# Fused graph attention and two-expert FFN on one core: another prologue, rstd by logarithm and exponential, and transposes and projection moved ahead of attention

## The chip, the core and the metric

The kernel runs on one core of a Trainium2 chip. The core's engines are TensorE (PE in the profile, PEld for its weight loads), VectorE (DVE), ScalarE (ACT), GpSimd (POOL) and SyncE (SP, which here only issues DMAs). Each engine executes its own list of instructions in order, and the lists meet only at semaphores. The metric is the device time of one execution in microseconds; lower is better.

## The reference

64 graphs of 128 nodes with 128 features each. First a graph attention layer, then a feed-forward layer in which each of the 8192 nodes uses its two most likely of 8 experts. Cut to what matters:

```python
h = layernorm(x);  Wh = h @ W                       # W 128 x 128
s1, s2 = Wh @ a1, Wh @ a2
e = leaky_relu(s1[:, :, None] + s2[:, None, :], 0.2)
x = x + softmax(where(adj > 0, e, -9e15), axis=2) @ Wh
h = layernorm(x)
probs = softmax(h @ gate_w + gate_b)                # 8 experts
top2_vals, top2_idx = top_k(probs, 2)
for e in range(8):                                  # weight 0 for experts not chosen
    out += cw[:, e] * (gelu(h @ W1[e] + b1[e]) @ W2[e] + b2[e])
x = x + out
```

## The kernel before

All is float32, in two stages. The **graph stage** (`NG` = 8 groups of `GB` = 8 graphs) does attention, the router, and a sort: every node's row is written to a DRAM table `sorted_rows` in a region for its pair of experts. The **expert stage** (`NT` = 91 tiles of 128 rows) reads 128 rows of one pair at a time, normalises, runs both experts and writes the rows back to their places.

Group g in the graph stage goes through these helpers. TensorE: `turn_x(g)` (eight 128x128 transposes of the input into the PSUM tile `q_ps`), `project(g)` (eight products with `w_ext` into `wh_ps`; it also gives the attention scores' two vectors and the gate's part), `score(g)` (a transpose of the two vectors, then masks and sums s1 + s2 into `q_ps`), `attend(g)` (eight transposes of the probabilities into `q_ps`, eight products with `wh` into `at_ps`), `count_ranks(g)` (places of the rows by counting, into `q_ps`). ScalarE copies each of them out of PSUM: `copy_xT`, `copy_wh` (which multiplies by rstd, the reciprocal standard deviation of the layernorm's input), `copy_s`, `copy_scores`, `copy_probsT`, `copy_rank`; it also does `exp`, `make_mask` and `exp_router`. VectorE: `split_s(g)` (the two vectors as high and low parts, which `score(g)` waits for), `softmax_shift(g)` (leaky relu and row maximum, `leaky` and `row_max`), `row_sums`, `x1` and `gates` (out of `at_ps`), the layernorm statistics (`stats_at_start` for groups 0 to 3, `of_x`, `of_x1`, `norms` in the loop), some twenty small router steps, and `slots`, `sum_slots`, `store_slots`, which give the row's place in the table (`pos`, line 755). GpSimd builds constants, computes rstd by a power of -0.5 (`rstd_of_start`, `rstd_of`, lines 276 and 328), and issues one indirect DMA (a scatter) of 128 rows per graph (`sort_rows`, line 319, 64 in all).

All three large users of `q_ps` share its two banks, so the order of the helpers on TensorE, and the same order on ScalarE, is written out by hand. Round i of the loop is on TensorE (lines 1091 to 1103) `score(i+1)`, `attend(i)`, `count_ranks(i-2)`, `turn_x(i+3)`, `project(i+3)`; on ScalarE (451 to 477) `copy_s(i+1)`, `exp(i)`, `copy_scores(i+1)`, `copy_probsT(i)`, `copy_wh(i+2)`, `copy_rank(i-2)`, `exp_router(i-1)`, `copy_xT(i+3)`, `make_mask(i+2)`; on VectorE (`rows_and_first(i)`, then `softmax_shift(i+1)`, `split_s(i+2)`, `norms_and_second(i)`). Round 0 differs: `score(1)`, `turn_x(2)` and `project(2)` come after `attend(0)`. Round i of VectorE begins with `row_sums(i, 0)` (line 579), which waits for the first three products of `attend(i)`.

The expert stage starts when all 64 scatters have landed (SP waits for `rows_sorted`, line 262) and the table of tiles is there.

Of the kernel before, what the change touches and what calls it, by code (L numbers as in the profile page):

```python
# [9 lines left out]
ALU = mybir.AluOpType  # L10
# [3 lines left out]
P = 128  # L14
# [20 lines left out]
WB = 3  # L35
# [4 lines left out]
def build(nc, x, adj, W, a, gate_w, gate_b, W1, b1, W2, b2, out, sorted_rows):  # L40
# [7 lines left out]
    with ExitStack() as ctx:  # L48
# [52 lines left out]
        minus_mean = sb("minus_mean", [P, GB, 2])  # L101
        rstd = sb("rstd", [P, 2, 2 * GB])
# [62 lines left out]
        rstd_ready = sem("rstd_ready")  # L165
# [43 lines left out]
        LN = 4  # L209
        RT = 20  # L210
# [9 lines left out]
        def _(sp):  # L220
# [21 lines left out]
            sp.dma_start(gb_row[:, :], gate_b.rearrange("(o e) -> o e", o=1).broadcast_to([P, E])).then_inc(gb_loaded, 16)  # L242
            sp.dma_start(experts[:, :, 0:B1], W1.rearrange("e d h -> d e h")).then_inc(experts_loaded, 16)
# [3 lines left out]
            b2_v = b2.rearrange("(o e) d -> o e d", o=1)  # L247
            sp.wait_ge(filled, 2)
            for k in range(3):
                sp.dma_start(b2_raw[32 * k:32 * k + 1, :, :], b2_v).then_inc(b2_loaded, 16)  # L250
            load_x(3)
            load_x(4)
# [20 lines left out]
        def _(pool):  # L273
# [22 lines left out]
            nc.gpsimd.memset(wh[:, :, :, WK:WK + 1], 1.0)  # L296
# [26 lines left out]
            def rstd_of(i):  # L323
                w = GB if i + 4 >= NG else 2 * GB
                pool.wait_ge(ln_step, LN * i + LN)
                if i >= 2:
                    pool.wait_ge(wh_ready, min(i + 3, NG))
                nc.gpsimd.tensor_tensor(rstd[:, i % 2, 0:w], stat[:, 5, 0:w], minus_half[:, 0:w], ALU.pow)\  # L328
                    .then_inc(rstd_ready, 1)

            for g in range(1, 4):
                rstd_of_start(g)
            for i in range(NG):
                if i >= 2:
                    pool.wait_ge(place_step, PL * (i - 1))
                    sort_rows((i - 2) * GB, (i - 2) * GB + 4)
                rstd_of(i)
                if i >= 2:
                    sort_rows((i - 2) * GB + 4, (i - 1) * GB)
            for i in range(NG - 2, NG):  # L340
                pool.wait_ge(place_step, PL * (i + 1))
                sort_rows(i * GB, (i + 1) * GB)
# [9 lines left out]
        def _(act):  # L352
# [14 lines left out]
            def copy_wh(g):  # L367
                act.wait_ge(wh_done, g + 1)
                if g < 4:
                    act.wait_ge(rstd_start_ready, g + 1)  # L370
                    by = rstd_start[:, g, :]
                else:
                    act.wait_ge(rstd_ready, g - 3)
# [44 lines left out]

            def exp_router(g):
# [9 lines left out]

            act.wait_ge(setup_pe, 2)  # L430
# [12 lines left out]
            copy_wh(0)  # L443
            copy_s(0)
            copy_scores(0, 0)
            copy_scores(0, 1)
            copy_xT(1, 0)
            copy_xT(1, 1)
            make_mask(1)

            for i in range(NG):
                if 1 <= i and i + 1 < NG:
                    copy_s(i + 1)
                exp(i)
                if 1 <= i and i + 1 < NG:
                    copy_scores(i + 1, 0)
                    copy_scores(i + 1, 1)
                copy_probsT(i, 0)
                copy_probsT(i, 1)
                if i == 0:  # L460
                    copy_wh(1)
                    copy_s(1)
                    copy_scores(1, 0)
                    copy_scores(1, 1)
                    copy_xT(2, 0)
                    copy_xT(2, 1)
                if i + 2 < NG:
                    copy_wh(i + 2)
# [4 lines left out]
                if i + 3 < NG:  # L473
                    copy_xT(i + 3, 0)
                    copy_xT(i + 3, 1)
# [712 lines left out]
```

## Time and profile before

| | us |
|---|---|
| median of 3 runs (409.86 to 411.43) | 411.04 |
| the profiled execution | 405.03 |
| its span in the trace | 403.0 |

| engine | busy us | share of the span | instructions |
|---|---|---|---|
| PE | 317.4 | 79% | 2354 |
| DVE | 242.9 | 60% | 1003 |
| ACT | 244.7 | 61% | 779 |
| POOL | 187.6 | 47% | 204 |

The graph stage takes the first 188 us or so of the span, the expert stage the rest. The time of an execution is 2.0 us more than the span of its trace. All times below are us from the span's start unless they are marked otherwise. The mean granted clock of TensorE over the span is 0.873 of full speed. In the chain of work that ended last, PE has 49% of the span, POOL 18% (the scatters of line 319 alone 12%, the rstd of line 328 4%) and DVE 11%.

### The profile page before, as it was taken

Reading aid. Unit: us, or ns where it says so; the run is one execution under the profiler, and the core shown is the slowest. Engines: PE = TensorE matmul, PEld = TensorE weight load, DVE = VectorE, ACT = ScalarE, POOL = GpSimd, SP = SyncE. Lnnn points to the kernel's source line nnn. Section 1 sums busy time; section 2 is a strip of 40 time slices with the busy share of each in tenths; the row PEclk is TensorE's granted clock in tenths of the full one; section 3 lists DMA queues with packets and bytes.
Section 4 is the critical chain, followed back from the end, with each engine's and each line's share of the span. In section 5 each row is a group of like instructions: output and inputs, shape, how many; then the busy total and the mean of one; then the engine's idle time right before and its main releaser. Section 6 shows DMA issues by size and latency. Waiting matters only on the chain.

```text
span 403.0 us, 9305 instructions
## 1 busy us (share of the span) xinstructions
PE 317.4 (79%) x2354; PEld 284.4 (71%) x2362; DVE 242.9 (60%) x1003; ACT 244.7 (61%) x779; POOL 187.6 (47%) x204
## 2 busy tenths in 40 slices
PE   7496797798775572210999999999999999999990
PEld 4274675675653461100999999899999999999980
DVE  4226879789788687640266565555566565565550
ACT  3354576576574320001888788787787877888850
POOL 5701410276766578772144444444444444444441
PEclk9868789969896865555899999999999999999996
DMA  7943003246921111111112222222222212212100
GB/s 206 306 124 85 21 0 107 66 119 140 164 50 47 34 36 47 54 55 47 38 46 58 53 59 58 65 57 64 54 69 61 61 47 51 57 51 57 47 3 0
DMA packets 42231, 27.85 MB, mean 69 GB/s; under 512 B 5224, under 2 KB 40070, under 8 KB 42182
## 3 DMA queue, kind: packets, MB, share of 16 engines
q1 hardware_dynamic: 37222, 18.69, 19.8%
q0 software_dynamic: 4960, 8.58, 7.2%
q8 instruction: 22, 0.36, 0.4%
q14 instruction: 27, 0.22, 0.2%
HBM read 16.78 MB, written 12.23 MB: 72 GB/s over the span
## 4 chain that ended last, share of the span: by engine, by line
PE 49%; POOL 18%; DVE 11%; issue 9%; DMA 6%; ACT 3%; SPq 1%; POOLq 0%; ACTq 0%; DVEq 0%
PE at_ps L1149 20%; PE wh_ps L1128 17%; POOL sorted_rows L319 12%; POOL rstd L328 4%; PE at_ps L1147 3%; DMA xt<-sorted_rows 3%; PE q_ps L1118 2%; DMA out_x<-o_sb,xt 2%; PE wh_ps L1018 2%; DVE rows L587 2%; DVE bn L607 1%; DVE bn L615 1%; ACT wh L381 1%; DVE lrelu L560 1%; PE q_ps L1042 1%
## 5 line engine op out<-in xcount | busy, mean ns | idle before, releaser
L346 POOL DMA_INDIRECT out_x<-o_sb,xt x91 | 89.0, 978 | 121.1 <-DVE o_sb L951 119.8
L500 ACT ACTIVATE hid<-wh_ps,pair_w 128x128 f32<-128x128 f32 x364 | 103.6, 369 | 16.9 <-PE wh_ps L1128 16.8
L1149 PE MATMUL at_ps<-experts,hid 128*128 x728 | 111.4, 288 | 0.0
L1128 PE MATMUL wh_ps<-xnT,pair_w 128*128 128x128 f32 x728 | 98.8, 279 | 0.0
L1149 PEld LDWEIGHTS at_ps<-experts,hid 128*128 128x128 f32 x728 | 95.9, 192 | 2.6
L1128 PEld LDWEIGHTS wh_ps<-xnT,pair_w 128*128 128x128 f32 x728 | 90.0, 195 | 0.2
L319 POOL DMA_INDIRECT sorted_rows<-rows,pos x64 | 63.3, 989 | 33.6 <-issue 17.3
L961 DVE COPY pair_w<-experts 128x258 f32 x182 | 54.2, 298 | 31.0 <-issue 18.4
L948 DVE SCALAR_TENSOR_TENSOR o_sb<-at_ps,xt 128x128 f32<-128x128 f32 x91 | 31.9, 351 | 67.3 <-PE at_ps L1149 67.1
L509 ACT ACTIVATE xn<-xt 128x128 f32<-128x128 f32 x91 | 44.5, 489 | 29.5 <-DMA xt<-sorted_rows 29.2
L1147 PE MATMUL at_ps<-experts,ones_bf 65*128 x182 | 40.9, 225 | 2.1 <-ACT hid L500 2.0
L1118 PE MATMUL q_ps<-ident,xn 128*128 128x128 f32 x91 | 25.4, 279 | 15.3 <-ACT xn L509 15.3
L951 DVE SCALAR_TENSOR_TENSOR o_sb<-at_ps,xt,o_sb 128x128 f32<-128x128 f32 x91 | 31.9, 351 | 3.2
L328 POOL TENSOR_TENSOR rstd<-stat,minus_half 128x16 f32<-128x16 f32 (+1 forms) x8 | 18.9, 2356 | 25.9 <-DVE stat L634 25.8
L490 ACT ACTIVATE xnT<-q_ps 128x128 f32<-128x128 f32 x91 | 25.3, 278 | 6.4
L1018 PE MATMUL wh_ps<-w_ext,xT 128*128 128x146 f32 x128 | 18.9, 302 | 8.0 <-ACT xT L364 8.0
L1118 PEld LDWEIGHTS q_ps<-ident,xn 128*128 128x128 f32 x91 | 13.1, 144 | 16.1 <-issue 15.3
L1018 PEld LDWEIGHTS wh_ps<-w_ext,xT 128*128 128x128 f32 x128 | 17.3, 200 | 9.8 <-issue 7.4
L1065 PE MATMUL at_ps<-wh,probsT 128*128 128x139 f32 x128 | 23.3, 351 | 0.3 <-ACT probsT L416 0.2
L1065 PEld LDWEIGHTS at_ps<-wh,probsT 128*128 128x128 f32 x128 | 22.0, 253 | 2.0 <-issue 1.4
L1147 PEld LDWEIGHTS at_ps<-experts,ones_bf 65*128 65x128 bf16 x182 | 18.0, 99 | 4.4 <-issue 4.1
L407 ACT ACTIVATE probs<-lrelu,less_max 128x128 f32<-128x128 f32 x64 | 19.5, 386 | 2.3 <-DVE less_max L565 2.3
(170 smaller groups left out, 390.0 us busy)
## 6 DMA issues: line engine op xcount, KB each, us to landing
xt<-sorted_rows SPq DMA_DIRECT2D x91, 66.5 KB
xin<-in_x SPq DMA_DIRECT2D x8, 512.0 KB, 4.6
adj_sb<-in_adj SPq DMA_DIRECT2D x8, 512.0 KB, 5.4
sorted_rows<-no_row SPq DMA_DIRECT2D x1, 1862.0 KB, 19.0
out_x<-o_sb,xt POOLq DMA_INDIRECT x91
experts<-in_L_ffn_W SPq DMA_DIRECT2D x1, 1024.0 KB, 6.8
experts<-in_L_ffn_W SPq DMA_DIRECT2D x2, 512.0 KB, 8.3
sorted_rows<-rows,pos POOLq DMA_INDIRECT x64
```

The source lines that it names most:

```text
L319: nc.gpsimd.indirect_dma_start(out=sorted_rows, out_offset=bass.IndirectOffsetOnAxis(ap=pos[:, t:t + 1], axis=0), in_=rows[:, t, :], in_of ...
L328: nc.gpsimd.tensor_tensor(rstd[:, i % 2, 0:w], stat[:, 5, 0:w], minus_half[:, 0:w], ALU.pow)\
L346: nc.gpsimd.indirect_dma_start(out=out_v, out_offset=bass.IndirectOffsetOnAxis(ap=xt[:, n % XR, TOK:TOK + 1].bitcast(I32), axis=0), in_=o_ ...
L500: last = nc.scalar.activation(hid[:, n % WR, q, :], wh_ps[:, n % WR, q * P:(q + 1) * P], ACT.Gelu, bias=pair_w[:, n % WR, k, B1 + c:B1 + c ...
L509: nc.scalar.activation(xn[:, n % 2, :], t[:, 0:P], ACT.Identity, bias=t[:, SHIFT:SHIFT + 1], scale=t[:, RSTD:RSTD + 1]).then_inc(xn_ready, 1)
L961: last = nc.vector.tensor_copy(pair_w[:, n % WR, k, :], experts[:, bass.ds(e, 1), 0:W2C])
L1018: last = nc.tensor.matmul(dst[:, o * WE:(o + 1) * WE], xT[:, k, :], w_ext[:, :], start=True, stop=True)
L1065: last = nc.tensor.matmul(dst[:, o * (WK + 1):(o + 1) * (WK + 1)], probsT[:, k, :], wh[:, g % WB, k, :], start=True, stop=True)
L1118: nc.tensor.transpose(q_ps[:, (n % 2) * 512:(n % 2) * 512 + P], xn[:, n % 2, :], ident[:, :]).then_inc(xnT_done, 1)
L1128: last = nc.tensor.matmul(wh_ps[:, n % WR, q * P:(q + 1) * P], pair_w[:, n % WR, k, c * P:(c + 1) * P], xnT[:, n % 2, :], start=True, stop ...
L1147: nc.tensor.matmul(at_ps[:, n % 2, cols], ones_bf[0:65, 0:P], b2_rows, start=True, stop=False)
L1149: last = nc.tensor.matmul(at_ps[:, n % 2, cols], hid[:, n % WR, k * HC + c, :], experts[:, bass.ds(e, 1), W2C + c * P:W2C + (c + 1) * P], ...
```

## The change

In the prologue (groups 0 to 2) the constants are no longer waited for before the statistics of group 1 and before `copy_wh(0)`; `turn_x` and `project` of groups 1 and 2, `score(1)` and group 3's transposes and projection all come before `attend(0)`. In the loop `turn_x(i+3)` and `project(i+3)` stand between `score(i+1)` and `attend(i)`, in every round; `wh` has 4 buffers instead of 3, and `copy_wh(i+3)` follows `copy_probsT(i)`. The power on GpSimd in the loop is replaced: ScalarE takes Ln and Exp (`rough_rstd`), VectorE one Newton step in four small operations (`exact_1` to `exact_4`) between the `x1` of the next round. The table set for Ln and Exp is named at the start and the one for Gelu loaded ahead of the expert stage. The splitting of `b2` goes from VectorE to GpSimd, and on SP the experts' weights are loaded after `x` of groups 3 and 4, `b2` and `adj` of group 2.

```diff
-WB = 3
+WB = 4
@@ sync
+            load_x(3)
+            b2_v = b2.rearrange("(o e) d -> o e d", o=1)
+            sp.wait_ge(filled, 2)
+            ... (three loads of b2)
+            load_adj(2)
+            load_x(4)
             (the three loads of experts)
-            (the three loads of b2), load_x(3), load_x(4)
-            for g in range(2, NG):
+            for g in range(3, NG):
                 load_adj(g)
-                if g + 3 < NG:
-                    load_x(g + 3)
+                if g + 2 < NG:
+                    load_x(g + 2)
@@ gpsimd
-            nc.gpsimd.memset(wh[:, :, :, WK:WK + 1], 1.0)
             for g in range(1, 4):
                 rstd_of_start(g)
-            for i in range(NG):
-                if i >= 2:
-                    pool.wait_ge(place_step, PL * (i - 1))
-                    sort_rows((i - 2) * GB, (i - 2) * GB + 4)
-                rstd_of(i)
-                if i >= 2:
-                    sort_rows((i - 2) * GB + 4, (i - 1) * GB)
-            for i in range(NG - 2, NG):
-                pool.wait_ge(place_step, PL * (i + 1))
-                sort_rows(i * GB, (i + 1) * GB)
+            (a memset and seven operations on b2, from the vector engine's list, each waiting for the last)
+            for g in range(NG):
+                pool.wait_ge(place_step, PL * (g + 1))
+                sort_rows(g * GB, (g + 1) * GB)
@@ scalar
-                if g == 0:
-                    act.wait_ge(consts, 14)          # in copy_wh
+            def rough_rstd(i):
+                w = GB if i + 4 >= NG else 2 * GB
+                act.wait_ge(ln_step, LN * i + LN)
+                nc.scalar.activation(log_var[:, 0:w], stat[:, 5, 0:w], ACT.Ln).then_inc(log_ready, 1)
+                act.wait_ge(log_ready, i + 1)
+                nc.scalar.activation(rough[:, 0:w], log_var[:, 0:w], ACT.Exp, scale=-0.5).then_inc(rough_ready, 1)
+            nc.scalar.preload_act_table_set("natural_log_exp_and_others")
             copy_xT(0, 1)
             make_mask(0)
             copy_wh(0)
+            copy_xT(1, 0)
+            copy_xT(1, 1)
             copy_s(0)
+            copy_wh(1)
             copy_scores(0, 0)
             copy_scores(0, 1)
-            copy_xT(1, 0)
-            copy_xT(1, 1)
+            copy_xT(2, 0)
+            copy_xT(2, 1)
             make_mask(1)
             for i in range(NG):
-                if 1 <= i and i + 1 < NG:
+                if i + 1 < NG:
                     copy_s(i + 1)
                 exp(i)
                 ... (copy_scores(i + 1, 0) and (i + 1, 1))
+                if i == 0:
+                    copy_wh(2)
+                if i + 3 < NG:
+                    copy_xT(i + 3, 0)
+                    copy_xT(i + 3, 1)
                 copy_probsT(i, 0)
                 copy_probsT(i, 1)
-                ... (round 0: copy_wh(1), copy_s(1), copy_scores(1), copy_xT(2))
-                if i + 2 < NG:
-                    copy_wh(i + 2)
+                if i >= 1:
+                    rough_rstd(i - 1)
+                if i + 3 < NG:
+                    copy_wh(i + 3)
                 ... (copy_rank(i - 2), exp_router(i - 1))
-                if i + 3 < NG:
-                    copy_xT(i + 3, 0)
-                    copy_xT(i + 3, 1)
                 ... (make_mask(i + 2))
+            nc.scalar.preload_act_table(ACT.Gelu)
             normalise(0)
@@ vector
+            exact_1: newton0 = stat5 * rough        exact_2: newton1 = newton0 * rough
+            exact_3: newton2 = 1.5 - 0.5 * newton1  exact_4: rstd = newton2 * rough
             def rows_and_first(i):
                 row_sums(i, 0)
+                exact_1(h)
                 x1(i, 0)
+                exact_2(h)
                 x1(i, 1)
+                exact_3(h)
                 x1(i, 2)
+                exact_4(h)
                 row_sums(i, 1)
                 gate_sum(h)
             stats_at_start(0)
+            nc.vector.memset(wh[:, :, :, WK:WK + 1], 1.0)
+            stats_at_start(1)
+            split_s(0)
+            stats_at_start(2)
+            split_s(1)
+            (leaky and row_max of group 0)
+            stats_at_start(3)
             dve.wait_ge(consts, 14)
             dve.wait_ge(gb_loaded, 16)
@@ tensor
             turn_x(0)
             project(0)
-            keep_busy(8)
-            score(0)
+            keep_busy(4)
             turn_x(1)
             project(1)
-            keep_busy(8)
+            score(0)
+            turn_x(2)
+            project(2)
             for i in range(NG):
-                if 1 <= i and i + 1 < NG:
+                if i + 1 < NG:
                     score(i + 1)
-                attend(i)
-                if i == 0:
-                    score(1)
-                    turn_x(2)
-                    project(2)
-                if i >= 2:
-                    count_ranks(i - 2)
                 if i + 3 < NG:
                     turn_x(i + 3)
                     project(i + 3)
+                attend(i)
+                if i >= 2:
+                    count_ranks(i - 2)
```

The waits that guard `q_ps` follow the new order (`turn_x(g)` waits for `copy_scores` of group g-2, `attend(g)` for `copy_xT(g+3)`). `preload_act_table_set` and `preload_act_table` load a table set of ScalarE at that place.

## Rows read from the trace of the kernel before

**Rows 1.** Windows view: length, busy PE, PEld, DVE, ACT, POOL, clock, DMA share, GB/s.
```profile
200.00:403.00 203.00, 191.33 (x1677) 186.36 (x1676) 114.52 (x353) 154.02 (x523) 87.98 (x90) 0.98 0.19 51
```
**Rows 2.** GpSimd's timeline: start, length, operation, in brackets idle before and releaser.
```profile
141.73 0.96 POOL L319 DMA_INDIRECT sorted_rows<-rows,pos  x1 [3.86 <-DVE pos L755]
...
158.35 1.68 POOL L328 TENSOR_TENSOR rstd<-stat,minus_half 128x8 f32<-128x8 f32 x1
...
183.04 0.96 POOL L319 DMA_INDIRECT sorted_rows<-rows,pos  x1 [0.30 <-issue]
184.30 0.96 POOL L319 DMA_INDIRECT sorted_rows<-rows,pos  x1 [0.30 <-issue]
```
**Rows 3.** ScalarE's timeline, start of the expert stage.
```profile
189.63 0.49 ACT L509 ACTIVATE xn<-xt 128x128 f32<-128x128 f32 x1 [13.68 <-DMA xt<-sorted_rows]
...
193.43 1.28 ACT L500 ACT_TABLE_LOAD   x1
...
194.73 1.14 ACT L500 ACTIVATE hid<-wh_ps,pair_w 128x128 f32<-128x128 f32 x4
```
**Rows 4.** VectorE's timeline, first instruction of rounds 0, 1, 4, 5, 6, 7.
```profile
33.37 0.18 DVE L579 RECIPROCAL rowinv<-at_ps 128x3 f32<-128x3 f32 x1 [5.88 <-PE at_ps L1065]
...
58.78 0.18 DVE L579 RECIPROCAL rowinv<-at_ps 128x3 f32<-128x3 f32 x1 [2.26 <-PE at_ps L1065]
...
102.62 0.18 DVE L579 RECIPROCAL rowinv<-at_ps 128x3 f32<-128x3 f32 x1
...
117.15 0.18 DVE L579 RECIPROCAL rowinv<-at_ps 128x3 f32<-128x3 f32 x1 [0.61 <-PE at_ps L1065]
...
134.01 0.18 DVE L579 RECIPROCAL rowinv<-at_ps 128x3 f32<-128x3 f32 x1 [3.86 <-PE at_ps L1065]
...
145.44 0.17 DVE L579 RECIPROCAL rowinv<-at_ps 128x3 f32<-128x3 f32 x1
```
**Rows 5.** VectorE's timeline inside rounds 1 and 4.
```profile
65.01 0.18 DVE L552 TENSOR_TENSOR s_cols<-wh,s_cols 128x16 fp32r<-128x16 f32 x1
...
105.60 0.18 DVE L654 TENSOR_TENSOR rows<-minus_mean,rstd 128x16 f32<-128x16 f32 x1 [1.81 <-POOL rstd L328]
```
**Rows 6.** TensorE's timeline: starts of its blocks (L1006 turn_x, L1034 score, L1057 attend, L978 filler).
```profile
8.14 1.07 PE L1006 MATMUL q_ps<-ident,xin 128*128 128x128 f32 x8
...
11.61 1.89 PE L978 MATMUL q_ps<-ones_bf 128*128 128x512 bf16 x7
...
24.87 1.97 PE L1006 MATMUL q_ps<-ident,xin 128*128 128x128 f32 x8
...
29.34 1.89 PE L978 MATMUL q_ps<-ones_bf 128*128 128x512 bf16 x8
31.07 1.04 PE L1057 MATMUL q_ps<-ident,probs 128*128 128x128 f32 x8
...
51.68 0.27 PE L1034 MATMUL q_ps<-ident,s_cols 128*32 128x128 f32 x1
...
55.22 1.94 PE L1057 MATMUL q_ps<-ident,probs 128*128 128x128 f32 x8
...
124.81 0.40 PE L1034 MATMUL q_ps<-ident,s_cols 128*32 128x128 f32 x1 [5.43 <-DVE s_cols L552]
...
130.57 1.97 PE L1057 MATMUL q_ps<-ident,probs 128*128 128x128 f32 x8
```
**Rows 7.** Busy time and granted clock by stretch, around rounds 1 and 5 (columns as Rows 1).
```profile
38.00:41.90 3.90, 3.90 (x13) 2.71 (x13) 3.46 (x21) 0.60 (x1) 1.93 (x2) 0.51 0.87 238
...
45.10:47.40 2.30, 2.30 (x20) 2.08 (x18) 2.30 (x13) 0.82 (x4) 0.00 (x0) 1.00 0.00 0
...
124.80:130.50 5.70, 4.86 (x14) 3.04 (x15) 5.14 (x37) 3.20 (x10) 3.23 (x4) 0.50 0.13 43
```
**Rows 8.** ScalarE's timeline: the copy of the first projection.
```profile
16.23 2.24 ACT L381 ACTIVATE wh<-wh_ps,rstd_start 128x138 f32<-128x138 f32 x8 [5.30 <-POOL part L315]
```

**Rows 9.** The source view of line 755, the rows' places: durations in ns, first and last start.
```profile
L755 DVE CAST pos<-pos_f x8: 151/152/171, 81.3 to 169.0; 128x8 int32<-128x8 f32 x8
```

More of the change, by code:

```diff
@@ L209, in build @@
         LN = 4
+        RS = 4
         RT = 20
@@ L634, in norms, with exact_1, exact_2, exact_3 @@
                 nc.vector.tensor_tensor(stat[:, 5, 0:w], stat[:, 3, 0:w], stat[:, 4, 0:w], ALU.add).then_inc(ln_step, 1)
+            def exact_1(i):
+                w = GB if i + 4 >= NG else 2 * GB
+                dve.wait_ge(rough_ready, i + 1)
+                nc.vector.tensor_tensor(newton[:, 0, 0:w], stat[:, 5, 0:w], rough[:, 0:w], ALU.mult).then_inc(rstd_step, 1)
+            def exact_2(i):
+                w = GB if i + 4 >= NG else 2 * GB
+                dve.wait_ge(rstd_step, RS * i + 1)
+                nc.vector.tensor_tensor(newton[:, 1, 0:w], newton[:, 0, 0:w], rough[:, 0:w], ALU.mult).then_inc(rstd_step, 1)
+            def exact_3(i):
+                w = GB if i + 4 >= NG else 2 * GB
+                dve.wait_ge(rstd_step, RS * i + 2)
+                nc.vector.tensor_scalar(newton[:, 2, 0:w], newton[:, 1, 0:w], -0.5, 1.5, ALU.mult, ALU.add)\
+                    .then_inc(rstd_step, 1)
+            def exact_4(i):
+                w = GB if i + 4 >= NG else 2 * GB
+                dve.wait_ge(rstd_step, RS * i + 3)
+                if i >= 2 and i + 2 < NG:
+                    dve.wait_ge(wh_ready, i + 3)
+                nc.vector.tensor_tensor(rstd[:, i % 2, 0:w], newton[:, 2, 0:w], rough[:, 0:w], ALU.mult).then_inc(rstd_step, 1)
             m1, k1, total, p1, e2, p2, k2, df, qa, qb, hi, lo, tri, cls = (small[:, j, :] for j in range(14))
@@ L827, in _ @@
             stats_at_start(0)
+            nc.vector.memset(wh[:, :, :, WK:WK + 1], 1.0)
[3 more added lines that the diff above has]
+            split_s(1)
+            for h in range(2):
+                leaky(0, h)
+                row_max(0, h)
+            stats_at_start(3)
             dve.wait_ge(consts, 14)
             dve.wait_ge(gb_loaded, 16)
-            stats_at_start(1)
-            split_s(0)
-            softmax_shift(0)
             for i in range(NG):
@@ L840, in _ @@
                     gates(0)
-                    split_s(1)
-                    stats_at_start(2)
-                    stats_at_start(3)
-                    softmax_shift(1)
+                else:
+                    rows_and_first(i)
+                if i + 1 < NG:
+                    softmax_shift(i + 1)
+                if i + 2 < NG:
+                    split_s(i + 2)
+                if i == 0:
                     for k in range(GB):
@@ L878, in _ @@
             store_slots(NG - 2)
+            exact_1(NG - 1)
+            exact_2(NG - 1)
+            exact_3(NG - 1)
+            exact_4(NG - 1)
             gate_sum(NG - 1)
```

103 lines of the change are left out of this document (38 added, 65 removed).

## The prediction, on record before the changed kernel was run

> **What bounds the kernel now.** I read the chain of work that ended last, then the timelines of the engines on it, then the windows. From 200 us on TensorE is busy 191 of 203 us [rows 1]: the expert stage is TensorE's, the change touches only its first instructions, and I carry it over as it is. It begins when the last scatter has landed: the last is issued at 184.30, and ScalarE waits until 189.63, 13.68 us long, for the first tile that is read back [rows 2, 3]. So the graph stage is worth what the last scatter is worth.
>
> GpSimd issues a scatter every 1.26 us [rows 2], 10.1 us for a group of eight, while the rounds of VectorE take longer: between the rounds' first instructions lie 25.4 us (round 0), 14.6 us on average (rounds 1 to 4), 16.9 (round 5) and 11.4 (round 6) [rows 4]. GpSimd therefore waits for each group's places until group 4, whose places come in round 6 and whose first scatter starts at 141.73, 7.7 us after the round's first instruction at 134.01 [rows 2, 4]. From then on it no longer waits: 32 scatters and two powers of 1.68 us and their issue to the end [rows 2]. So the end of the stage is "start of round 6 plus 50.3 us", and what matters before is how fast the rounds go.
>
> A round is a ring. VectorE's first instruction waits for `attend(i)`; 6.4 us later (58.78 to 65.19 [rows 4, 5]) `split_s(i+2)` is done; that releases `score(i+2)` on TensorE, then `attend(i+1)`, which releases the next round. The second half of the ring is 3.54 us of score (51.68 to 55.22) plus 2.30 us of attend (31.07 to 33.37) at the full clock, and 5.76 (124.81 to 130.57) plus 3.44 (130.57 to 134.01) at the half clock [rows 4, 6]. Meanwhile VectorE has about 7 us of statistics and router work of its own, so in rounds 2 to 4 the two sides are nearly level. `turn_x` and `project` run now beside the first half of the ring, while TensorE waits for `split_s`: they cost nothing.
>
> **The change, part by part.**
>
> *Transposes and projection between score and attention.* They leave the free place and enter the ring. The two blocks take 3.47 us at the full clock (8.14 to 11.61) and 4.47 us at the half (24.87 to 29.34), ScalarE's copies between them included [rows 6]. `attend(i)` is queued behind them, VectorE's round waits for `attend(i)`, everything else for that. This falls on the rings that lead to rounds 1 to 4; the later rounds have no group left to turn. What they leave behind is a hole: TensorE ends `attend` and `count_ranks` some 2.7 us into a round and has nothing until `split_s`.
>
> The clock decides how dear it is. At 124.81 TensorE had idled 5.43 us, and score ran at a granted clock of 0.50, that is 1.2 GHz [rows 6, 7]. Score does not bring it back either: at 38.0 to 41.9 TensorE is busy all the time with score and is at 0.51; transposes and projection follow until about 46, and the full 2.4 GHz is back at 45.1 to 47.4 [rows 7]. In the new order every score follows an idle of about 4.5 us. I take 5.3 us for score (bounds 3.54 and 5.76, nearer the half clock), 4.4 for turn and project (3.47 and 4.47), 2.6 for attend (2.30 and 3.44, the clock mostly back): 12.3 us, bounds 9.3 and 13.7.
>
> *rstd by Ln and Exp.* Two powers after 141.73 leave GpSimd's list, and VectorE's wait for them (1.81 us in round 4 [rows 5], between 0 and that in the others) goes. In their place VectorE has four small operations, at about 0.1 us each from start to start in a stream of such, 0.18 at most [rows 5]: 0.4 us per round. `exact_1` waits for ScalarE, where Ln and Exp (at most 0.28 us each, the mean of the eight copies in [rows 8]) stand behind `copy_probsT(i)`; they end about when VectorE starts its round. Bounds 0 and 0.8 us of stall, queued behind it the `x1` of the round; I take 0.3, since the products that release VectorE come after the same copy. `copy_wh(i+3)` waits for `exact_4`, 1.6 us into the round; behind it wait `copy_rank`, `exp_router` and `make_mask`, all needed only after the first half of the ring. So the first half becomes 6.45 + 0.7 = 7.15 us, and the new round 7.15 + 12.3 = 19.45 against 14.6. VectorE's own list (7.15 + 7) is shorter and is now hidden.
>
> *Prologue.* `copy_wh(0)` sat idle for 5.30 us until 16.23 for constants it does not need [rows 8]; now it can run at 11.85, when `project(0)` is done [rows 6]. But more stands ahead of `attend(0)`. Following TensorE and ScalarE: `copy_wh(0)` to 14.3 (2.4 us with its two small copies), the first half of `copy_xT(1)` 0.6, `project(1)` to 17.1, `score(0)` to 20.9, `turn_x(2)` and `project(2)` to 24.9, half of it at the half clock, `score(1)` to 28.6, `turn_x(3)` waits for `copy_scores(1)`, then ScalarE does `copy_wh(2)` (2.4) before `copy_xT(3)` (0.6 for its first half), `project(3)` from 32.2 to 34.9, attend 2.6: round 0 starts at 37.5. With every block at the full clock it is 36.4, at the half 42.5. Before: 33.37 [rows 4]. Round 0's first half is short (no router), rows 3.0, shift 2.45, split 0.4 = 5.85 us, then 12.3: round 1 starts at 55.65, against 58.78. The prologue gains 3.1 us there, because groups 1 and 2 are ready, not more, since `turn_x(4)` and `project(4)` are in the ring.
>
> *Gelu's table ahead of time.* The load of 1.28 us at 193.43 is on the path [rows 3] and moves into the 13.68 us in which ScalarE waits: -1.3 us. The Trainium skill (ScalarE: Activation LUTs, What ACT_TABLE_LOAD costs) counts 2.66 us per switch with a drain. By the page the gain would be 1.4 us larger. In the trace the activation behind the load starts at 194.73, 0.02 us after the load's end [rows 3], so I keep 1.3.
>
> *b2 on GpSimd, loads in another order, memset, filler.* Nothing. GpSimd's first scatter will not come before about 84 us (the first places came at 81.3 [rows 9]), and between the starting rstd and that it has only b2's eight operations; even at three times 1.68 us each they would end by 70 us. VectorE loses them in round 0, where it idled anyway until 58.78 [rows 4]. All loads that move forward are needed later than they land.
>
> **The sum.** Rounds start at 37.5, 55.65, then three times 19.45: round 4 at 114.0 (before 102.62). Round 5: 7.15 + 9.2 (score and attend at the half clock, as 124.81 to 134.01) = 130.4; round 6 likewise, 146.8 (before 134.01). Group 4's first scatter comes 7.7 + 0.7 = 8.4 us later, and 31 more at 1.263 = 39.15 behind it: the last starts at 194.4, against 184.30 [rows 2]. That is +10.1, less 1.3 for Gelu: +8.8 us. Group 7's places came at 169.0 [rows 9], 35 us into round 6; with 8.9 us to their last scatter's start that is 44 against 47.6, so they don't bind. The profiled execution would take 405.03 + 8.8 = 413.8; the runs' median is 6.0 above it, so I add the same to the median: 411.04 + 8.8 = 419.8 us.
>
> **Rivals.**
> 1. *The clock stays at 2.4 GHz, and the kernel is faster.* Transposes and projections beside score could feed TensorE enough. With all blocks at the full clock: round 0 at 36.4, 1 at 51.6, three rounds of 7.15 + 9.3 to 101, two of 13.0 (VectorE's own work then, 12.6, is nearly level) to 127.0; last scatter 174.6, -9.7, with Gelu -11.0: 400. For it: round 5 began after an attend at the full clock (117.15). Against: the idle of 4.5 us in every round, and score at the half clock even when it is busy [rows 7]. The ring's second half decides: it must be under 10.1 us instead of 12.3 for the change to break even. 10%.
> 2. *The clock comes back in mid-ring more often.* Second half about 10.3 us: round 6 at 139, the end within 2 us of before: 412. 9%.
> 3. *Ln and Exp don't stay in one table set with the sign, copy and exp of the loop.* Then 1.28 us [rows 3] per switch, two a round in ScalarE's list, half of it ahead of `exact_1`: 7 x 1.3 to 2.6 us more, 429 to 438. The Trainium skill (ScalarE: Activation LUTs, Table sets: the hidden batching unit) says one set has both Ln and Exp and that cheap functions are in every set; by it this rival is nothing. 5%.
> 4. *The half clock holds through attend too*: second half 13.7 and a prologue with round 0 at 42.5: +19: 430. The Trainium skill (TensorE: Matmul & The Clock Gate, PE-mode transpose) says transposes don't count as activity for the clock, which would speak for it; the trace shows eight transposes of the input in 1.07 us at one place and 1.97 at another [rows 6], so they at least run at the full clock where it is granted. 6%.
>
> **How the numbers follow.** The forecast, a ring of 11 to 13.5 us and a result of 414 to 427, has 70%. About 0.5% (2 us) is what a measurement of this kernel can tell from no change. Faster by more: 10% (rival 1). Within: 8%, most of rival 2. Slower: 82%. The range reaches down into rival 2 and up short of rivals 3 and 4: 409.5 to 427.
>
> **What would show it.** In the trace after: the first instructions of rounds 1 to 5 should lie 18 to 20.5 us apart; before each `score` TensorE should idle 4 to 5 us for `split_s`, and VectorE 4 us or more before each round for `attend`; score at 0.5 to 0.7 of the clock; round 1 at 54 to 57; no wait of VectorE for rstd over 0.8 us; GpSimd without a wait in its last 32 scatters; a single table load before the experts. It is wrong if the rounds come at 16.5 us or less (clock), if round 0 starts before 35, or if ScalarE loads tables in the loop.

## The result, and the profile after

Over four runs the changed kernel takes 421.24 us (419.73 to 422.48), beside 410.45 us for the kernel before on the same chip (four runs, 405.21 to 411.43). The ratio is 1.031, its 95% interval 1.020 to 1.041: slower, by about 3%. The forecast was 419.8 us with a range of 409.5 to 427.

The traces say more than +10.8 us. The profiled execution of after took 420.99 us with a span of 419.0, against 405.03 and 403.0 of before, so trace to trace it is +16.0 us, where +8.8 had been worked out. The last scatter went from 184.30 [rows 2] to 201.09: +16.8, and -0.8 behind it. The median was met partly by luck, because two errors cancel: the graph stage lost 6.7 us more than predicted, and the profiled execution of before lies 5.4 us below the median of its own runs, while that of after lies on its median.

The page of after, granted clock, the chain and one group:

```profile
PEclk9965775768685656555579999999999999999996
...
PE 61%; DVE 11%; POOL 10%; issue 7%; DMA 5%; ACT 3%; SPq 1%; POOLq 0%; ACTq 0%; DVEq 0%
...
L598 DVE RECIPROCAL rowinv<-at_ps 128x3 f32<-128x3 f32 (+1 forms) x24 | 4.1, 172 | 53.8 <-PE at_ps L1092 53.6
```

TensorE's share of the chain rose from 49% to 61%, GpSimd's fell from 18% to 10%. The third to the twentieth digit of the clock's line (a slice is 10.5 us) lie between 5 and 8: TensorE is rarely at its full speed in the graph stage. The last line is the round's first instruction: VectorE waits 53.6 us in all before this line, for `attend`.

VectorE's timeline of after, the first instruction of rounds 0 to 6, answers [rows 4]:

```profile
40.88 0.18 DVE L598 RECIPROCAL rowinv<-at_ps 128x3 f32<-128x3 f32 x1 [15.02 <-PE at_ps L1092]
59.99 0.18 DVE L598 RECIPROCAL rowinv<-at_ps 128x3 f32<-128x3 f32 x1 [9.37 <-PE at_ps L1092]
80.37 0.18 DVE L598 RECIPROCAL rowinv<-at_ps 128x3 f32<-128x3 f32 x1 [7.51 <-PE at_ps L1092]
100.74 0.18 DVE L598 RECIPROCAL rowinv<-at_ps 128x3 f32<-128x3 f32 x1 [6.75 <-PE at_ps L1092]
121.13 0.18 DVE L598 RECIPROCAL rowinv<-at_ps 128x3 f32<-128x3 f32 x1 [6.83 <-PE at_ps L1092]
137.32 0.18 DVE L598 RECIPROCAL rowinv<-at_ps 128x3 f32<-128x3 f32 x1 [4.07 <-PE at_ps L1092]
153.62 0.18 DVE L598 RECIPROCAL rowinv<-at_ps 128x3 f32<-128x3 f32 x1 [4.07 <-PE at_ps L1092]
```

The starts of rounds 1 to 4, with a transposition and a projection between each two, follow each other at 20.4 us instead of 14.6 [rows 4]; once no group is left to turn it is 16.2 and 16.3. VectorE idles 6.8 to 7.5 us at the end of each of the long ones.

TensorE's timeline of after from one round's start to the next (80.37 to 100.74), the first instruction of each block (L1061 score, L1036 turn_x, L1048 project, L1084 attend), answers [rows 6]:

```profile
87.14 0.28 PE L1061 MATMUL q_ps<-ident,s_cols 128*32 128x128 f32 x1 [4.54 <-DVE s_cols L571]
...
92.78 1.97 PE L1036 MATMUL q_ps<-ident,xin 128*128 128x128 f32 x8
94.68 3.85 PE L1048 MATMUL wh_ps<-w_ext,xT 128*128 128x146 f32 x16
98.37 1.04 PE L1084 MATMUL q_ps<-ident,probs 128*128 128x128 f32 x8
```

And the windows of after over the same stretches: the hole before score, score, turn and project, attend (columns as [rows 1]), which answer [rows 7]:

```profile
83.00:87.00 4.00, 0.00 (x0) 0.00 (x0) 3.97 (x16) 2.65 (x9) 0.00 (x0) 1.00 0.43 129
87.10:92.80 5.70, 4.83 (x15) 3.05 (x16) 5.70 (x38) 3.20 (x10) 2.85 (x3) 0.56 0.38 115
92.80:98.40 5.60, 5.60 (x26) 5.26 (x26) 1.08 (x8) 1.79 (x3) 4.14 (x5) 0.54 0.16 52
98.40:100.80 2.40, 2.06 (x19) 1.85 (x17) 0.06 (x1) 1.40 (x4) 0.96 (x1) 1.00 0.19 57
```

So a ring is 6.77 us to the start of score, 5.64 of score, 5.59 of turn and project, 2.37 to the next round's start: 20.37. TensorE is empty for 4.54 us, then busy for 11 us at little over half its clock, and is given the full clock only where `attend` begins. While it turns and projects, VectorE is busy 1.08 us of 5.60: nothing else is left to do then.

GpSimd's timeline of after, group 4's first scatter and the last, answers [rows 2]:

```profile
161.76 0.95 POOL L325 DMA_INDIRECT sorted_rows<-rows,pos  x1 [6.21 <-DVE pos L796]
...
201.09 0.96 POOL L325 DMA_INDIRECT sorted_rows<-rows,pos  x1 [0.30 <-issue]
```

The last 32 scatters still run without a wait, now 39.3 us from first to last instead of 42.6, since the two powers are gone. The end of the stage is still "start of round 6 and a fixed list", which makes the rounds the thing to explain.

### The profile page after: what moved, and what is told of

Same layout as the page of the kernel before. It is cut to its first block, busy times and chain, and to the rows that moved or that the text cites. A ratio compares the mean times of both kernels' runs of the same rounds, so it can differ in the third digit from the quotient of the medians.

```text
span 419.0 us, 9314 instructions
## 1 busy us (share of the span) xinstructions
PE 327.7 (78%) x2343; PEld 295.8 (71%) x2350; DVE 240.2 (57%) x1028; ACT 248.7 (59%) x795; POOL 177.8 (42%) x203
## 4 chain that ended last, share of the span: by engine, by line
PE 61%; DVE 11%; POOL 10%; issue 7%; DMA 5%; ACT 3%; SPq 1%; POOLq 0%; ACTq 0%; DVEq 0%
PE at_ps L1173 19%; PE wh_ps L1152 17%; POOL sorted_rows L325 7%; PE wh_ps L1048 5%; DVE rows L606 3%; PE at_ps L1092 3%; PE at_ps L1171 3%; PE q_ps L1072 2%; PE q_ps L1069 2%; PE q_ps L1036 2%; DVE lrelu L579 2%; DMA xt<-sorted_rows 2%; PE q_ps L1142 2%; PE q_ps L1084 2%; PE q_ps L1067 2%
## 5 line engine op out<-in xcount | busy, mean ns | idle before, releaser
L325 POOL DMA_INDIRECT sorted_rows<-rows,pos x64 | 61.8, 965 | 101.9 <-DVE pos L796 84.2
L598 DVE RECIPROCAL rowinv<-at_ps 128x3 f32<-128x3 f32 (+1 forms) x24 | 4.1, 172 | 53.8 <-PE at_ps L1092 53.6
L1048 PE MATMUL wh_ps<-w_ext,xT 128*128 128x146 f32 x128 | 27.9, 397 | 3.4 <-ACT xT L375 3.4
L1048 PEld LDWEIGHTS wh_ps<-w_ext,xT 128*128 128x128 f32 x128 | 26.2, 286 | 5.6 <-ACT x_gate L393 3.6
L1061 PE MATMUL q_ps<-ident,s_cols 128*32 128x128 f32 x8 | 2.6, 323 | 27.7 <-DVE s_cols L571 27.7
L1092 PE MATMUL at_ps<-wh,probsT 128*128 128x139 f32 x128 | 22.4, 341 | 1.4 <-ACT probsT L425 1.4
L1092 PEld LDWEIGHTS at_ps<-wh,probsT 128*128 128x128 f32 x128 | 21.0, 243 | 3.0 <-issue 2.8
L1142 PEld LDWEIGHTS q_ps<-ident,xn 128*128 128x128 f32 x91 | 13.2, 145 | 13.5 <-issue 12.6
L1061 PEld LDWEIGHTS q_ps<-ident,s_cols 128*32 128x32 f32 x8 | 0.8, 98 | 29.7 <-DVE s_cols L571 29.7
```

What stands on the lines that cost most here:

```text
L325: nc.gpsimd.indirect_dma_start(out=sorted_rows, out_offset=bass.IndirectOffsetOnAxis(ap=pos[:, t:t + 1], axis=0), in_=rows[:, t, :], in_of ...
L1048: last = nc.tensor.matmul(dst[:, o * WE:(o + 1) * WE], xT[:, k, :], w_ext[:, :], start=True, stop=True)
L1092: last = nc.tensor.matmul(dst[:, o * (WK + 1):(o + 1) * (WK + 1)], probsT[:, k, :], wh[:, g % WB, k, :], start=True, stop=True)
L1142: nc.tensor.transpose(q_ps[:, (n % 2) * 512:(n % 2) * 512 + P], xn[:, n % 2, :], ident[:, :]).then_inc(xnT_done, 1)
```

## Experiments

The theories, as the expectations name them: **A**, the place in the ring (turn and project between score and attention cost their length, and make the hole in front of score in which the clock goes); **C**, the clock alone (the blocks would be nearly harmless if TensorE stayed warm). The other parts of the change are tested one by one. "Before" is always the run of the kernel before on the same chip. Differences between two experiments are of medians, and where no ratio stands they are told with their ranges.

### Only the order undone

```diff
@@ tensor (and ScalarE's list in the same order, with the waits that guard q_ps)
                 if i + 1 < NG:
                     score(i + 1)
-                if i + 3 < NG:
-                    turn_x(i + 3)
-                    project(i + 3)
                 attend(i)
                 if i >= 2:
                     count_ranks(i - 2)
+                if i + 3 < NG:
+                    turn_x(i + 3)
+                    project(i + 3)
@@ scalar
-                (copy_xT(i + 3) ahead of copy_probsT(i), copy_wh(i + 3) behind it)
+                (copy_wh(i + 2) behind copy_probsT(i), copy_xT(i + 3) after exp_router)
```

> The changed kernel with one part undone: in the loop turn_x(i+3) and project(i+3) stand again behind attend(i) and count_ranks(i-2), with ScalarE's copies in the same order; prologue of groups 0 to 2, rstd by Ln and Exp, b2, loads and Gelu's table stay. Theory A (the two blocks in the ring cost the loop its time): rounds 1 to 3 fall from 20.4 us to about 14.2, VectorE's own list; round 0 starts near 33 instead of 40.9, since attend(0) no longer stands behind turn_x(3) and project(3), round 4 near 90, the last scatter at about 168; total 390 to 398 us, below the kernel before. Rival B (the new prologue, the split rstd or the waits make the loop slow, the place of the two blocks is a detail): the rounds stay over 17 us and the total at 412 or more.

387.89 us (387.22 to 388.18, 4 runs) beside 408.4 (404.52 to 411.18): ratio 0.951, 0.944 to 0.958. All else of the change is still in. So the order costs 33.4 us of the changed kernel's 421.24 (32.9 between the spans of the two traces, 419.0 and 386.1), and the rest of the change gains 20.5; the two don't add up to the 10.8 measured, because the medians of before beside them, 410.45 and 408.4, differ by 2.0. A held: the rounds and the last scatter (168.62) came where it put them, the total 2 us below its range. The first instructions of rounds 0, 1, 3, 4 and 6 on VectorE:

```profile
31.36 0.18 DVE L596 RECIPROCAL rowinv<-at_ps 128x3 f32<-128x3 f32 x1 [5.45 <-PE at_ps L1088]
48.68 0.18 DVE L596 RECIPROCAL rowinv<-at_ps 128x3 f32<-128x3 f32 x1 [4.87 <-PE at_ps L1088]
...
77.17 0.18 DVE L596 RECIPROCAL rowinv<-at_ps 128x3 f32<-128x3 f32 x1
91.04 0.18 DVE L596 RECIPROCAL rowinv<-at_ps 128x3 f32<-128x3 f32 x1
...
121.04 0.18 DVE L596 RECIPROCAL rowinv<-at_ps 128x3 f32<-128x3 f32 x1 [3.84 <-PE at_ps L1088]
```

Rounds 2 to 4 take 13.8, 13.9 and 14.1 us. Rounds 3 and 4 begin with no wait: VectorE's own list has become the bound. TensorE in round 3:

```profile
82.11 2.23 PE L1048 MATMUL wh_ps<-w_ext,xT 128*128 128x146 f32 x16 [0.34 <-ACT xT L375]
84.32 0.28 PE L1060 MATMUL q_ps<-ident,s_cols 128*32 128x128 f32 x1
...
87.86 1.73 PE L1080 MATMUL q_ps<-ident,probs 128*128 128x128 f32 x8
```

`project` ends as score begins: the hole of 4.54 us is filled by the blocks, which cost nothing there and keep the clock up, so that score takes 3.54 us instead of 5.64. This ring is 7.15 + 3.54 + 3.18 = 13.87 against 6.77 + 5.64 + 5.59 + 2.37 = 20.37. Of the 6.50 between them, 5.59 are the blocks in the ring and 2.10 score's clock. Against that, the fast ring is 0.81 us longer from attend on (attend is partly at the half clock, 0.65 from 87.8 to 91.1, and VectorE's own list ends only just before 91.04) and 0.38 in the first half, 0.32 of it a wait of VectorE for Exp. The prologue tells the same: round 0 starts 9.52 us earlier, at 31.36 instead of 40.88. Group 3's blocks, which no longer stand ahead of `attend(0)`, are 7.66 of them; 1.25 lie ahead of these blocks, most of it in `project(2)`, which met a higher clock (2.80 us instead of 4.00), and 0.61 in attend.

### The changed order with a warm TensorE

```diff
+            def fill(count):
+                for _ in range(count):
+                    nc.tensor.matmul(q_ps[:, 512:1024], ones_bf[:, 0:P], ones_bf[:, :], start=True, stop=True)
@@ tensor, at the head of round i
+                if i >= 1 and i + 1 < NG:
+                    fill(20)
                 if i + 1 < NG:
                     score(i + 1)
```

> The changed kernel with 20 filler products of 512 bf16 columns (4.3 us at the full clock) ahead of score(i+1) in rounds 1 to 6, where TensorE idles 3.8 to 5.6 us for split_s; nothing of the result changes. Theory A says the ring is long mainly by the blocks in it and the score drops the clock by itself: score begins at the full clock, but turn_x and project behind it run partly at the half; rounds of 18 to 19.5 us instead of 20.4, total 408 to 417. Rival C (the idle before score is the whole cause of the half clock): score 3.55, turn and project 3.5, attend 2.4, rounds of 16.2 us, total 400 or less. If the filler delays score it costs as much as it overlaps split_s.

407.79 us (402.21 to 409.55, 4 runs) beside 408.4; the changed kernel has 421.24, and the ranges don't touch: -13.4 us, and about level with before. Two of the four runs lie at 402.2 and 406.6 and two near 409, so the median itself is loose; between the traces it is -14.3 us (spans 404.7 and 419.0). TensorE's timeline, rounds 2 and 3 starting at 74.80 and 92.18, and the windows of score and of turn and project:

```profile
76.86 4.48 PE L1028 MATMUL q_ps<-ones_bf 128*128 128x512 bf16 x20
81.58 0.28 PE L1065 MATMUL q_ps<-ident,s_cols 128*32 128x128 f32 x1 [0.23 <-DVE s_cols L571]
...
85.12 1.79 PE L1040 MATMUL q_ps<-ident,xin 128*128 128x128 f32 x8
86.76 3.22 PE L1052 MATMUL wh_ps<-w_ext,xT 128*128 128x146 f32 x16
89.81 1.04 PE L1088 MATMUL q_ps<-ident,probs 128*128 128x128 f32 x8
```

```profile
81.60:85.10 3.50, 3.14 (x15) 1.83 (x16) 3.50 (x24) 3.08 (x10) 1.23 (x1) 1.00 0.50 146
85.10:89.80 4.70, 4.69 (x25) 4.26 (x25) 3.23 (x22) 1.79 (x3) 3.57 (x4) 0.64 0.19 61
```

The ring fell from 20.4 to 17.4 us: 2.10 in score, which is now at the full clock, and 0.90 in turn and project, which are not: they run at 0.64 although TensorE had been filled and then kept busy. C wanted 16.2 us and 400 or less, A 18 or more and 408 at least; it came between, nearer A. So what the fillers gave back of the clock is 3.0 us of a ring, and with that the ring is still 3.5 us longer than with the order undone. Had the blocks too run at the full clock, where they take 3.47 us [rows 6] for these 4.69, another 1.2 would have gone; that was not reached in any run. Both theories hold a share; neither alone is right.

### rstd: the power on GpSimd, in each order

The kernel after with the power of the kernel before in place of Ln, Exp and the Newton step:

```diff
-                if i >= 1:
-                    rough_rstd(i - 1)            # ScalarE: Ln, Exp
-                (exact_1 to exact_4 between the x1 of VectorE)
+            def rstd_of(i):                      # GpSimd, between sort_rows
+                ...
+                nc.gpsimd.tensor_tensor(rstd[:, i % 2, 0:w], stat[:, 5, 0:w], minus_half[:, 0:w], ALU.pow)
```

> The changed kernel with rstd by the power on GpSimd as before, in the places that it had among the scatters (Ln, Exp and the Newton step gone). Theory: in rounds of 20 us the power (2.9 or 1.7 us) is hidden in VectorE's idle time before the round, 0.4 us of Newton work per round go (-2.5 in all), and GpSimd's last 32 scatters have two powers among them (+3.3): between 0 and +3 us. Rival: the power delays copy_wh and with it the ring: +8 or more.

421.85 us (421.29 to 422.65, 6 runs), ratio 1.035, 1.029 to 1.040. That is 0.6 us above the changed kernel: inside 0.5%, no difference. That is in the 0 to +3 us expected. In its trace the power is in GpSimd's list again and the last scatter is at 203.34 instead of 201.09. `split_s` ends 0.31 us earlier in each of the long rounds, since the four Newton steps no longer stand before it (its last instruction starts 6.23 us into the round instead of 6.54), and the rounds are no shorter for it, 20.5 us: in round 2 score (86.4 to 92.3) and the two blocks were granted 0.50 throughout. The window of the two blocks (columns as [rows 1]):

```profile
92.20:98.10 5.90, 5.90 (x26) 5.55 (x26) 0.92 (x8) 1.79 (x3) 5.04 (x4) 0.50 0.08 26
```

Here they take 5.91 us to the start of attend, and `project` alone 4.18.

The same edit on the kernel with the order undone:

> e1_order with rstd by the power on GpSimd, so the kernel before plus the new prologue, b2, loads and Gelu's table, without Ln and Exp. It splits the 20 us that e1_order lies below the kernel before. Theory: the prologue (round 1 of VectorE at 48.7 instead of 58.8) is 10 to 12 us of it; the rest is rstd (two powers out of GpSimd's last 32 scatters 3.3 us, VectorE's waits for rstd in rounds 2 to 4, 4 us, less 3 of Newton steps): 391 to 396 us. Rival: the prologue's gain is lost again in the loop and nearly all comes from rstd: 402 or more.

397.38 us (394.97 to 399.0, 4 runs), ratio 0.969, 0.964 to 0.975; 391 to 396 had been expected. This is 9.5 us above the kernel with only the order undone (387.89), which ran on another chip; against the later runs of that kernel on this chip (386.61, below) it is 10.8. Between the traces the span is 8.0 us longer, and 6.6 of it are there at the last scatter, on GpSimd's timeline at 175.18 against 168.62.

```profile
175.18 0.96 POOL L323 DMA_INDIRECT sorted_rows<-rows,pos  x1 [0.30 <-issue]
```

Of those 6.6, 3.4 are round 6, which starts at 124.41 instead of 121.04, and 3.2 the two powers (1.67 us each) in front of the last scatters. The same edit makes no difference that can be told where the ring has 7 us of slack for VectorE, and 8 to 11 us where it has none. It also splits the gain of 20.5 roughly: prologue, loads and the rest 12.6 (409.99 to 397.38), rstd 9.5; taken on two chips, they add up to 22.1. What the prologue, the loads and `b2` are worth one by one was not tested.

### Gelu's table loaded where it is needed

```diff
-            nc.scalar.preload_act_table(ACT.Gelu)
```

> The changed kernel without the early load of Gelu's table. Theory: the load of 1.28 us stands again between the first activations of the experts, +1.3 us. By the table page of the Trainium skill (a switch with its drain) +2.7 us. Rival: the first tiles wait for their DMAs anyway, 0.

420.37 us (419.85 to 423.22, 6 runs), ratio 1.033, 1.027 to 1.039. Against 421.24 (419.73 to 422.48) no difference can be told, where +1.3 us had been expected, so on the total this is inconclusive. ScalarE's timeline, the first row read back, the load, the first `hid`:

```profile
204.85 0.49 ACT L527 ACTIVATE xn<-xt 128x128 f32<-128x128 f32 x1 [11.25 <-DMA xt<-sorted_rows]
...
208.66 1.28 ACT L518 ACT_TABLE_LOAD   x1
209.95 1.14 ACT L518 ACTIVATE hid<-wh_ps,pair_w 128x128 f32<-128x128 f32 x4
```

From the first `xn` to the first `hid` it is 5.10 us; in the kernel after, with the load at 195.47 inside a wait, 4.02 (206.40 to 210.42). So 1.08 us left this stretch.

### Best of both: the order undone, and fillers where TensorE still idles

With the order undone TensorE still waits for `split_s` where no block, or a block already done, stands beside the ring's first half: 3.68 us before `score(2)` and 4.09 before `score(7)`. The expectation names `score(6)` as a third such place; in the trace of that kernel TensorE waits only 0.18 us there.

```diff
@@ on top of the kernel with the order undone
+                if i in (1, 5, 6):
+                    fill(14)
                 if i + 1 < NG:
                     score(i + 1)
```

> e1_order with 14 filler products of 512 bf16 columns (3 us at the full clock) ahead of score(2), score(6) and score(7), the places where TensorE still idles 3.7 to 4.1 us for split_s. If the idle is what drops the clock, rounds 0 and 5 fall from 17.3 to about 15 and from 15.9 to about 13.8, round 4 stays at VectorE's list; total 382 to 386 us against 387.9. If score at the full clock does not shorten them, 387 to 389.

387.43 us (385.15 to 389.72, 6 runs), ratio 0.945, 0.940 to 0.950: no different from 387.89, and above the 382 to 386 expected. Rounds 0 and 5 became shorter (13.3 and 14.4 us, from 17.3 and 15.9), but round 4 longer, 16.3 from 14.1: `project(7)` comes directly ahead of that filler, so there it fills no hole and stands in the ring. Hence the version with `i in (1, 6)`:

> e6_order_fill without the filler ahead of score(6): the trace of e6_order_fill shows that TensorE had no idle there (project(7) ends when split_s does), so those 3 us of filler stood in the ring and the round that leads to 5 took 16.3 us instead of 14.1. With filler ahead of score(2) and score(7) alone that round is 14.1 again, and rounds 0 and 5 keep 13.3 and 14.4: 384 to 386 us. Rival: the clock then falls at another place and it stays at 387 to 389.

and on the same chip the kernel with only the order undone again:

> e1_order once more, on the same chip as e8_order_fill2, so that the two can be compared: 387 to 389 us.

With two fillers it is 385.33 us (384.55 to 385.81, 6 runs), ratio 0.946, 0.941 to 0.951, without 386.61 (385.56 to 389.03, 6 runs), ratio 0.951, 0.945 to 0.956; before 408.12 for both. The one lies within the 384 to 386 expected, the other just below its 387 to 389. TensorE's timeline of the version with two fillers, `score(2)` and `attend(1)`:

```profile
41.05 0.27 PE L1064 MATMUL q_ps<-ident,s_cols 128*32 128x128 f32 x1
...
44.58 1.40 PE L1084 MATMUL q_ps<-ident,probs 128*128 128x128 f32 x8
```

and the same stretch of TensorE without fillers:

```profile
39.85 0.28 PE L1060 MATMUL q_ps<-ident,s_cols 128*32 128x128 f32 x1 [3.48 <-DVE s_cols L569]
...
44.62 1.97 PE L1080 MATMUL q_ps<-ident,probs 128*128 128x128 f32 x8
```

`score(2)` takes 3.53 us instead of 4.77, and round 0 is 13.3 us instead of 16.7: 1.24 of it in score, 1.26 in attend, 0.89 in the first half. But round 0 starts at 33.70 instead of 31.61, before any filler stands in the list; the last section has the windows on that. The last scatter comes 3.9 us earlier (163.43 against 167.34) but the span is only 1.0 shorter (383.1 against 384.1): in the expert stage TensorE is busy 164.8 of the 175 us from 205 on, instead of 168.0. The chain of that run has more DMA in it (10% against 5%). What gave the 2.9 us back stays open. It is the fastest kernel of the study, 22.8 us under before, though its lead over the one without fillers (1.3 us, ranges that touch) is at the limit of what can be told.

### The kernel before, profiled once more

> The kernel before, unchanged, with a second profile, since the first (405.03 us) is one of its faster executions. If the spread of its runs (404.5 to 411.4) is TensorE's clock falling at another place, a slower execution shows one or two rounds with score or attend at the half clock that had the full clock in the first profile, 2 us each; if it is the expert stage, the graph stage is the same within 1 us.

This execution was a fast one again, so it doesn't answer what a slow one looks like. 406.07 us, span 404.1, last scatter at 185.70, rounds' starts within 2.1 us of those of [rows 4]. So the trace of before on which the sum rests is repeatable, and is one of the faster executions of that kernel, whose runs went from 404.5 to 412.3 us over the chips used here; those near 411 have no trace. Over the 33 executions taken beside the experiments the mean granted clock is 0.849 to 0.858 in the six above 411 us and 0.858 to 0.874 in the five below 406, so by and large the longer ones had the lower clock; in which stage it falls stays open.

## Why the prediction was right, and where it wasn't

**The mechanism was right.** VectorE's round waits for `attend`, `attend` stood behind the blocks, and TensorE found a hole of 4.5 us before each score. The order undone alone gave 33.4 us back. Rival 1 (the clock stays) falls by the windows at 0.56 and 0.54 and by rounds of 20.4 us, rival 2 (second half 10.3 us) by a second half of 13.60. Of the signs named, one failed: round 1 was to start at 54 to 57 and started at 59.99.

**The term that was mis-sized: turn and project.** They were put at 4.4 us, with 4.47 as the upper bound "at the half clock", and took 5.59. The bound wasn't one: the rows 24.87 to 29.34 [rows 6] are of a stretch in which the clock had come back on the way. TensorE in the kernel before, by single microseconds (busy time, clock, DMA share, GB/s):

```profile
27.00:28.00 1.00, 1.00 (x6) 0.59 0.00 0
28.00:29.00 1.00, 1.00 (x11) 1.00 0.00 0
```

Wholly at the half clock the two blocks take 5.91 us (the window at 0.50 above) and `project` alone 4.18 (4.23 in the prologue, its window 0.50), against 2.23 at the full clock. A block between two time stamps is a bound for one clock only if the window over it shows that clock all through. The other terms were near: score 5.64 for 5.3, attend 2.37 for 2.6, the first half 6.77 for 7.15. The second half was 13.60 for 12.3: inside the 13.7 that had been given as its bound, and just outside the 11 to 13.5 that had been given 70%. Three rings at 20.38 for 19.45 are 2.8 us of the 6.7 missed.

**The prologue was mis-sized too, by 4.3 us.** Round 0 was forecast at 37.5 (36.4 to 42.5) and came at 40.88, round 1 at 55.65 and came at 59.99. The forecast gave group 3's two blocks 2.7 us for `project(3)`, behind a turn taken at the full clock. TensorE's timeline of after:

```profile
22.71 4.00 PE L1048 MATMUL wh_ps<-w_ext,xT 128*128 128x146 f32 x16
...
30.18 1.97 PE L1036 MATMUL q_ps<-ident,xin 128*128 128x128 f32 x8
33.81 4.23 PE L1048 MATMUL wh_ps<-w_ext,xT 128*128 128x146 f32 x16 [1.67 <-ACT xT L375]
37.84 1.91 PE L1084 MATMUL q_ps<-ident,probs 128*128 128x128 f32 x8
```

Turn, wait and projection of group 3 fill 7.66 us before `attend(0)`, all at the half clock (windows at 0.50), and attend begins at it (its window is at 0.66). The 3.1 us that the prologue was to gain at round 1 became a loss of 1.2. That it does gain, without those blocks in it, the order undone shows: round 1 at 48.68 instead of 58.78 [rows 4]. `copy_wh(0)` was freed as forecast; it ran at 11.22 instead of 16.23 [rows 8]:

```profile
11.22 2.24 ACT L390 ACTIVATE wh<-wh_ps,rstd_start 128x138 f32<-128x138 f32 x8 [0.89 <-PE wh_ps L1048]
```

**The rest.** From the start of round 4 to that of round 6 it took 32.5 us for 32.8, group 4's first scatter came 8.14 us into round 6 for 8.4, the 31 behind it took 39.3 for 39.15. The four Newton steps cost 0.31 us of the first half (6.54 us to the last instruction of `split_s` against 6.23 with the power), for 0.4 forecast, and no stall: in round 1 Exp, on ScalarE's timeline at 59.48, ends before VectorE's first step of the four at 60.09.

```profile
59.48 0.22 ACT L433 ACTIVATE rough<-log_var 128x16 f32<-128x16 f32 x1
```

```profile
60.09 0.14 DVE L657 TENSOR_TENSOR newton<-stat,rough 128x16 f32<-128x16 f32 x1
```

The 0.3 us of stall per round was not there in the slow ring (one wait of 0.43 us, after round 7); in the fast ring of the order undone it is, 0.32 us in round 3 and 0.42 in round 4. The sum priced the powers' removal in GpSimd's list only; it did not ask what it would be worth in a fast ring, where it is 8 to 11 us. Rival 3 (tables switched in the loop) is refuted: the trace has two table loads, at 0.79 and at 195.47. The Trainium skill (ScalarE: Activation LUTs, Table sets: the hidden batching unit) says that one set holds both exp and ln, and the trace agrees. Gelu moved 1.08 us off the path by the trace of the kernel without the early load, and 0.8 between the traces of before and after; 1.3 was forecast. The Trainium skill (ScalarE: Activation LUTs, What ACT_TABLE_LOAD costs) counts a drain on top of the load; in both traces with the load on the path the activation behind it starts within 0.02 us of its end, so nothing of a drain is seen.

**Rival 4** (the half clock through attend too) was half true: in the prologue the transposes of `attend(0)` run at it, in the loop the windows give attend 1.00. The Trainium skill (TensorE: Matmul & The Clock Gate, PE-mode transpose) holds that the full clock doesn't engage for transposes. Here the eight transposes at 98.37 take 1.04 us, in a window at 1.00, and the eight at 92.78 take 1.97 us at 0.54: they follow the clock that is granted.

**The median.** 405.03 + 16.0 is 421.0; the median of before had been taken as 6.0 us above its profile and the same added to after. It wasn't there: the four runs of after lie within 3 us of each other, around the profiled one. The hit within 1.4 us of the median is thus luck in its size: 8.8 + 6.0 stood for a true 16.0 + 0.2. The chance of slower, 82%, rests on the mechanism and is not touched by this.

## What to carry to other kernels

A block that fills an engine's wait is free where it stands; moved between two steps that the other engines wait for, it cost its whole length here, at the clock that it met there, and left a hole behind which the next step ran slower (33 us in all). Price each block at both clocks from windows that show one clock throughout, and let a forecast's base be an execution that lies at the median of its runs, or say by how much it may be off. The worth of any other edit, such as the power of rstd, depends on which wait ends last: nothing that could be told in the slow ring, 8 to 11 us in the fast one.

## What the hardware showed that was not expected

The clock falls behind score even where TensorE did not idle before it. In the version with fillers score is entered at full clock and runs at 1.00, TensorE is busy 3.14 of its 3.50 us and without a break after it, and still turn and project get 0.64. With the order undone attend gets 0.65 behind a score at 1.00. Where TensorE idles before score, the clock does not fall at one place: in rounds 2 and 3 of the changed kernel it stays at 1.00 through a hole of 4.5 us and falls within the first 1.2 us of score; in round 1 it falls inside the hole, where TensorE has no product at all:

```profile
63.00:66.70 3.70, 0.00 (x0) 0.00 (x0) 3.67 (x14) 2.00 (x7) 0.00 (x0) 0.62 0.50 146
```

What the grant follows these runs don't settle.

The same list can meet another clock. Up to 34 us the kernel with two fillers and the one without have the same instructions on TensorE in the same order, and `turn_x(2)` starts at 20.95 in both. The windows from 24 to 32, without and with fillers:

```profile
24.00:28.00 4.00, 3.64 (x22) 2.62 (x21) 1.79 (x11) 2.41 (x9) 1.95 (x2) 0.93 0.59 166
28.00:32.00 4.00, 3.85 (x27) 3.10 (x27) 0.35 (x2) 3.61 (x10) 3.72 (x4) 1.00 0.02 5
```

```profile
24.00:28.00 4.00, 3.64 (x17) 2.90 (x17) 1.79 (x11) 1.66 (x6) 1.96 (x2) 0.71 0.59 163
28.00:32.00 4.00, 4.00 (x20) 3.07 (x20) 0.00 (x0) 3.16 (x9) 3.73 (x4) 0.72 0.03 7
```

The one is granted 0.93 and 1.00 where the other gets 0.71 and 0.72, and that is the 2.1 us between their rounds 0. A difference of 2 us between two single traces is therefore no evidence for an edit; the 6.5 us per ring and the 33 us of the order are far above it.

An operation of VectorE can stand still beside one of GpSimd. Off the critical path, in the prologue of after:

```profile
11.72 1.86 DVE L556 SCALAR_TENSOR_TENSOR stat_start<-stat_start 128x8 f32<-128x8 f32 x1
```

```profile
11.52 2.03 POOL L299 TENSOR_SCALAR_AFFINE_SELECT selector<-selector_raw 32x2048 fp32r<-32x2048 f32 x1
```

A step on 128x8 elements, whose neighbours take 0.16 to 0.20 us (in the first fence VectorE, in the second GpSimd), took 1.86 us and ended with GpSimd's selection of 2.03 us. The traces of the other eight runs with this prologue have such a step there too, always one, 1.86 to 2.01 us long and ending within 0.04 us of the selection. Which step it is changes, even between two runs of one kernel: it is a TENSOR_TENSOR, a SCALAR_TENSOR_TENSOR or a TENSOR_SCALAR. No run varied the selection, so what makes the step wait is argued from the ends alone.
